# Filler matmuls in TensorE's waits: an attention block and a quantised feed-forward block in one program

## What is computed

```
x = x + attention(layernorm(x), ctx, ctx, Wq, bq, Wk, bk, Wv, bv, Wo, bo)    # 16 heads of 32, RoPE on q and k, causal
x = x + ffn(layernorm(x), w_gate, w_up, w_down)                              # inner size 1536

def act_qdq(x):                                  # one scale for the whole tensor
    scale = jnp.maximum(jnp.max(jnp.abs(x)) / 32767, 1e-12)
    return jnp.clip(jnp.round(x / scale), -32768, 32767) * scale

def ffn(x, w_gate, w_up, w_down):                # lpbq_dequant: 4 bits, one scale for each 32 weights
    x = act_qdq(x)
    up = act_qdq(x @ lpbq_dequant(w_up).T)
    gate = act_qdq(x @ lpbq_dequant(w_gate).T)
    sig = fixed_qdq_u16(jax.nn.sigmoid(gate))
    gate = act_qdq(gate * sig)
    o = act_qdq(gate * up)
    return o @ lpbq_dequant(w_down).T
```

## Time and profile before

| what | us |
|---|---|
| median of three runs | 1491.33 |
| the profiled execution, its own time | 1493.25 |
| its span | 1491.5 |
| TensorE busy with matmuls | 1371.2 (92% of the span) |
| VectorE busy | 1182.0 (79%) |
| ScalarE busy | 968.2 (65%) |
| GpSimd busy | 342.6 (23%) |

### The profile page before, as it was taken

How to read it: one execution, slowest core, us unless ns; L and a number is a source line. 1 busy time by engine, 2 the same in 40 slices (tenths; PEclk the granted TensorE clock), 3 DMA queues, 4 the chain that set the end, 5 groups by cost and what they waited for, 6 DMA issues and landing times.

```text
span 1491.5 us, 24413 instructions
## 1 busy us (share of the span) xinstructions
PE 1371.2 (92%) x9186; PEld 772.7 (52%) x9186; DVE 1182.0 (79%) x1793; ACT 968.2 (65%) x2027; POOL 342.6 (23%) x326
## 2 busy tenths in 40 slices
PE   5899999999999999979999999999999408999999
PEld 4566666667666766643444444444444203444444
DVE  6878888888898888747788987898899899565541
ACT  6988888898888888746422222999889894222210
POOL 0544455444455454430111111000000000000000
PEclk9999999999999999989999999999999758999999
DMA  6111121211121111114533333677689999577632
GB/s 230 48 58 58 65 69 53 72 71 72 72 72 58 58 43 44 37 55 143 190 117 130 134 109 117 234 247 261 240 298 321 388 397 372 201 235 237 236 99 85
DMA packets 101557, 224.75 MB, mean 151 GB/s; under 512 B 8768, under 2 KB 21184, under 8 KB 99776
## 3 DMA queue, kind: packets, MB, share of 16 engines
q1 hardware_dynamic: 100864, 219.00, 41.4%
q10 hardware_dynamic: 576, 4.19, 0.8%
HBM read 140.32 MB, written 82.84 MB: 150 GB/s over the span
## 4 chain that ended last, share of the span: by engine, by line
PE 49%; issue 4%; DVE 1%; ACT 0%; POOLq 0%; POOL 0%
PE ffn_banks L1275 32%; PE ffn_banks L1292 17%; DVE ffn_wide L1484 0%; DVE ffn_peaks L1491 0%; DVE qg L1614 0%; DVE ffn_rises L1489 0%; DVE ffn_wide L1483 0%; ACT qg L1346 0%; ACT ffn_wide L1346 0%; PE ffn_banks L1283 0%; DVE ffn_wide L1645 0%; DVE ffn_wide L1673 0%; ACT ffn_ring L1325 0%; DVE ffn_rest L1612 0%; DVE ffn_peaks L1499 0%
## 5 line engine op out<-in xcount | busy, mean ns | idle before, releaser
L1275 PE MATMUL ffn_banks<-ffn_wide,ffn_rest 128*128 128x512 f16 x2304 | 500.1, 380 | 3.7 <-DVE ffn_wide L1479 2.7
L1275 PEld LDWEIGHTS ffn_banks<-ffn_wide,ffn_rest 128*128 128x128 f16 x2304 | 225.8, 98 | 277.8 <-issue 3.4
L1292 PE MATMUL ffn_banks<-ffn_rest,ffn_wide 128*128 128x512 f16 x1152 | 250.6, 381 | 63.2 <-DVE ffn_wide L1649 63.2
L640 ACT ACTIVATE qg<-score_banks,neg_max 128x128 f32<-128x128 f32 (+1 forms) x512 | 208.2, 450 | 20.8 <-DVE neg_max L512 20.8
L1292 PEld LDWEIGHTS ffn_banks<-ffn_rest,ffn_wide 128*128 128x128 f16 x1152 | 113.0, 98 | 200.8 <-issue 66.1
L1444 ACT ACTIVATE ffn_u_steps<-ffn_ring,ffn_scales 128x1024 int16<-128x1024 f32 x48 | 55.0, 1148 | 153.4 <-DMA ffn_ring<-ups_dram 133.4
L417 POOL TENSOR_TENSOR qg<-qg,per_sum 128x512 f32<-128x512 f32 x64 | 85.9, 1342 | 269.7 <-DVE per_sum L516 269.7
L1346 ACT ACTIVATE ffn_rest<-ffn_banks,ffn_row_back 128x1024 f32<-128x1024 f32 x66 | 73.0, 1105 | 95.2 <-PE ffn_banks L1275 91.5
L419 POOL TENSOR_TENSOR qg<-qg,per_sum 128x1024 f32<-128x1024 f32 x64 | 133.7, 2088 | 0.0
L640 ACT ACTIVATION_READ_ACCUMULATOR qg<-score_banks,neg_max 128x1 f32 x512 | 121.1, 237 | 0.0
L649 ACT ACTIVATE pt<-ring_banks 128x512 f32<-128x512 f32 x128 | 70.4, 610 | 41.9 <-PE ring_banks L776 41.0
(11 more groups left out here) (198 smaller groups left out, 2695.6 us busy)
## 6 DMA issues: line engine op xcount, KB each, us to landing
ffn_ring<-ups_dram SPq DMA_DIRECT2D x44, 512.0 KB, 5.7
ups_dram<-ffn_rest SPq DMA_DIRECT2D x42, 512.0 KB, 3.7
ffn_wide<-ups_dram SPq DMA_DIRECT2D x13, 1024.0 KB, 14.0
gates_dram<-ffn_rest SPq DMA_DIRECT2D x24, 512.0 KB, 2.7
ffn_ring<-gates_dram SPq DMA_DIRECT2D x24, 512.0 KB, 4.6
signs_dram<-qg SPq DMA_DIRECT2D x24, 512.0 KB, 4.2
qg<-signs_dram SPq DMA_DIRECT2D x48, 256.0 KB, 7.2
ffn_rest<-w_parts_dram SPq DMA_DIRECT2D x36, 256.0 KB, 4.4
```

The source lines that it names most:

```text
L640: last = act.activation(prob[:, s % 2, h, lo:hi], score_banks[:, h, lo:hi], ACT.Exp, bias=neg_max[:, s % 2, part, h:h + 1], accum_out=row_ ...
L1275: last = pe.matmul(banks[:, pair_of(s), half, :], w[:, m % 2, wp, c, :], xq[:, xp, n, c, :], start=(k == 0), stop=(k == 3 * DC - 1))
L1292: last = pe.matmul(down_banks[:, g % 2, t, :], oq[:, g % 2, op, m, t * P:(t + 1) * P], w_down[:, wp, wk, c], start=(start and k == 0), sto ...
```

## The change

A function `turn_over(bank, times)` issues so many matmuls one after the other. Each multiplies a 128x128 block of the matrix of ones, read as bfloat16, with 256 columns of the same tile, and writes 256 columns of a PSUM bank that nobody reads before it is written anew. None of them waits for another engine except where written, and none signals one. They stand at six places of TensorE's program, 130 in all: 22 ahead of the first `QK`, 10 ahead of the first `V`, 18 ahead of the last `PT` (after a new wait for the last exponentials), 26 after the last `O`, 18 after the matmul that spreads the input's maximum, and 36 ahead of the down projection (after a new wait for 22 of the 24 product units). In `QK` and `V` the waits are reordered: the wait for a free bank now stands first.

```diff
+        unused = ones[:, :].bitcast(BF16)
...
+            def turn_over(bank, times):
+                for _ in range(times):
+                    pe.matmul(bank, unused[:, 0:P], unused[:, :], start=True, stop=True)
...
                 if name == "QK":
+                    b = open_bank("QK", g, i)
+                    if i == 0 and g == 0:
+                        turn_over(banks[:, b, 0:SEQ], 22)
...
-                    b = open_bank("QK", g, i)
...
                 if name == "V":
+                    b = open_bank("V", g, i)
+                    if i == 0 and g == 1:
+                        turn_over(banks[:, b, 0:SEQ], 10)
...
-                    b = open_bank("V", g, i)
...
                 if name == "PT":
+                    if s == BATCH * GROUPS - 1:
+                        pe.wait_ge(exped, s + 1)
+                        turn_over(score_banks[:, 3, 0:SEQ], 18)
                     pe.wait_ge(normed, s + 1)
...
                     if name == "O":
                         last.then_inc(last_filled, 1)
+                        if g == 1:
+                            turn_over(score_banks[:, 3, 0:SEQ], 26)
...
             pe.matmul(banks[:, 3, 0, 0:P], keep["ones"][:, :], spread, start=True, stop=True).then_inc(top_spread, 1)
+            turn_over(banks[:, 2, 0, 0:2 * P], 18)
...
                 if g < 2:
                     pe.wait_ge(staged, 2 * NP)
+                    if g == 0:
+                        pe.wait_ge(u_peaked, ND - 2)
+                        turn_over(banks[:, 3, 1, 0:2 * P], 36)
```

More of the change, by code:

```diff
@@ L980, in feed_forward @@
         block = ctx.enter_context(nc.Block())
+        unused = keep["ones"][:, :].bitcast(BF16)
         first, second = chain_slots()
```

## The result

| | before | changed |
|---|---|---|
| median of 10 runs | 1491.61 us | 1483.26 us |
| lowest to highest | 1488.55 to 1496.18 | 1482.03 to 1488.15 |
| profiled execution | 1493.25 | 1482.14 |

The ratio is 0.9948, with a 95% interval of 0.9934 to 0.9963: faster by 5 to 10 us. The forecast was 1485.9 with a range of 1482.5 to 1490.3, so the time lies in the range, 2.6 us under the point. The two profiled executions differ by 11.1 us, more than the medians do.

A forecast was written before the change was run, and what follows sets the result against it. TensorE was taken to bound the kernel from 692 us to the end. The terms 1.98 + 1.2 + 1.7 + 0.45 + 0.2 + 1.8 = 7.3 us came off the profiled 1493.25, giving 1485.9, range 1482.5 to 1490.3.

The forecast's parts named there:

- Part 1: 22 fillers ahead of the first QK: QK0 2.2 us shorter, gain capped at 1.98 us by VectorE's wait for ScalarE.
- case of a late rise: Ahead of the first QK: a clock rise 1.2 us later leaves 5 or 6 products cold, gain 1.4 us.
- Part 2: 10 fillers ahead of the first V: V1 at full clock, exponentials sooner, gain 1.2 us, 0 to 1.5.
- Part 3: 18 fillers ahead of the last PT: transposes and Oc at full clock, 1.7 us where the clock fell, otherwise 0.
- Part 4: 26 fillers after the last O: the second four YT transposes at full clock, 0.45 us, or 0.
- The rule of the Trainium skill: At YT's transposes: transpose-mode matmuls don't count as work, so the clock falls after the 26 fillers; sum 6.65, time 1486.6.
- Part 5: Spreading matmul faster if the clock stands, even odds, 0.2 us; the 18 fillers after it worth 0, -0.7 to +0.1.
- Part 6: 36 fillers ahead of the down projection: its first 3.6 us at full clock, gain 1.8 us, up to 2.4.
- The first rival: Attention's rhythm gives back the early gains of 3.2 us: 1489.1 us, chance 0.15.
- The second: Fillers raise the clock but do not hold it; only first QK and down projection gain, 3.8 us: 1489.5, chance 0.1.
- The slow one: At all six places each filler waits for the one before to drain: 10.5 us slower, 1503.7 us, chance 0.05.
- a microsecond that TensorE saves at the head of either stretch is a microsecond of the end: From 692 us: TensorE bounds gate and up products, 477 us, and down projection, 250.6 us, unless another engine sets the head.

The follow-up runs named there:

- e1: The kernel before with only the 22 fillers ahead of the first QK and the 10 ahead of the first V: ratio 0.9977, 3.4 us.
- e3: The kernel before with only the 36 fillers ahead of the down projection: ratio 0.9981, 2.8 us.
- e9: The changed kernel without the 18, 26 and 18 fillers around the border of attention and the feed-forward part: ratio 0.9957.
- e5: The changed kernel with 36 transposes in place of the 36 fillers ahead of the down projection: clock rose 6.0 us after the start; no time given.
- e4: The changed kernel without the 18 fillers after the spreading matmul: ratio 0.9954.
- e8: The changed kernel with 8 more fillers ahead of the last sequence's first PV and 12 ahead of its third S: ratio 0.9941.
- e6: The changed kernel with 72 fillers ahead of the down projection in place of 36: 1486.97 us, one run.
- e7: The changed kernel with 18 fillers ahead of the down projection in place of 36: 1489.41 us, one run.
- e2: The kernel before with only the 18, 26 and 18 fillers around the border of attention and the feed-forward part: ratio 1.0008.
- after_again: The changed kernel measured a second time: ratio 0.9946.
- e10: The changed kernel with 8 and 12 more fillers near the end of attention and 14 ahead of the second sequence's first S: ratio 0.9955.

## Why the prediction was right, and where it was off

1. *Part 1, 1.98 us*: right in size (1.96 at the rotation, 2.1 at 38.6 us) and in mechanism. `QK0` now waits 0.85 us for its operands after the fillers and takes 2.6 us instead of 4.8 (its 24 starts lie between 21.65 and 24.16). The rotation starts with no idle time before it: VectorE's own work ahead of it has become the limit, as the cap of 1.98 us said. The clock rose sooner than the 21.2 us I had put: the fillers' spacing drops from 0.213 to 0.109 us at 19.5, 2.6 us after the first of them (1.5 to 4.3 in the eleven profiles that have the 22). My case of a late rise was added up wrongly: a rise 1.2 us later leaves 3 products cold, not 5 or 6, and a gain of 1.7 us, not 1.4. That the gain is carried to the end is shown by e1.
2. *Part 2, 1.2 us*: mis-sized; the stretch gave 1.7. I let VectorE's wait of 1.23 us for ScalarE cap it. VectorE's reciprocal took all of that (51.01 to 47.59, -3.42), but at 55.00, the next score maximum, the saving was 3.81. That one had waited for TensorE, whose 3.4 us at half clock (43.17 to 46.59) cost it 1.7. I also took the fall at 43 to be one that only some executions have. It came in all three profiles that have no fillers there, at 43.2, 43.5 and 43.6, and in none of the eleven that have them.
3. *Part 3, 1.7 us, where the clock falls*: the size was right to 0.1 us, and so was the condition. Of the three other profiles in which the last `PT` runs without fillers and so could show it (e1, e3, e9), none had a fall there. So a fall came in one of four such profiles, and that the one I added up from had it was luck: for the median, this part was worth less than I put in.
4. *Part 4, 0.45 us*: 0.46, and in every profile: from the last `otlo` to the first instruction of the feed-forward part it is 9.35 or 9.36 us in the four without these fillers, and 8.89 or 8.90 in the ten with them. The clock stood through `YT`'s transposes, and it fell only at 661.3. The rule of the Trainium skill that the prediction weighed ("TensorE: Matmul & The Clock Gate", part 4) had been taken to make this 0; it came out at 0.46. The place itself does not decide on the rule, since the clock fell soon after. e5 does not agree with it: there the clock rose while nothing but float32 transposes ran.
5. *Part 5, 0.2 us and the fillers 0*: 0.31 and 0.1. The 0.31 needs the clock to stand until the spreading matmul has run, and it did so in 3 of the 10 profiles with the 26 fillers (the changed kernel, e4 and e8), in place of the even odds I gave it. e4 shows the cover by VectorE.
6. *Part 6, 1.8 us*: 1.8 (250.6 to 248.8 us busy). e3 shows it alone, e6 the price of a filler beyond the cover, e7 that half the number gave nothing.

The score maximum of point 2, in the kernel before, with its wait for TensorE:

```profile
55.00 0.69 DVE L511 TENSOR_REDUCE neg_max<-score_banks 128x4 f32<-128x512 f32 x1 [1.18 <-PE score_banks L765]
```

The first rival, that attention gives the early gain back, is refuted by e1. The second, that fillers raise the clock but don't hold it, is refuted by the fall at 43, which came without the 10 fillers each time and never with them, and by the 0.46 us of part 4. The slow one, that fillers do not follow each other closely, is refuted by their spacing: the 26 take 3.00 us, 0.109 us from start to start. Its sum held a slip of 0.2 us: 26 x 0.27 is 7.0, 3.3 us late and not 3.1.

One step failed, though the time came out in the range: that from 692 us on "a microsecond that TensorE saves at the head of either stretch is a microsecond of the end". For the first of the two stretches, the pieces, it holds for the profiled execution of before, and for three of the others, not in general. That explains how e2's profile could be 4.3 us ahead after the border and 0.1 at the first product unit, and it puts 1.07 us of loss into the profile of the changed kernel, which the pass over products then happened to give back. Against this went 3.0 us inside attention that I had no term for: 1.7 for a fall at 633.7 which no filler touches and which was absent, and 1.3 gathered in small steps between 55 and 520 us.

The largest of those steps, 0.85 us at 207 us, is one VectorE instruction (L507, L508 in the changed kernel) that took 2.80 us before and 1.96 after, where its median is 0.69. Beside it GpSimd was adding a bias (L405, from 204.66 to 207.02 before; L406, from 199.95 to 202.32 after), and VectorE's instruction ended 0.55 us later than that in both. The 14 profiles hold 162 cases in which this instruction takes over 0.8 us. In each it starts while that addition of GpSimd runs, and ends 0.54 to 0.56 us after it. So VectorE is held until GpSimd is done, and the size of the step is how long GpSimd still had to run (2.26 us before, 1.41 after). The instruction before and after:

```profile
204.76 2.80 DVE L507 SCALAR_TENSOR_TENSOR qg<-turns,sin_turned 128x512 f32<-128x512 f32 x1
200.91 1.96 DVE L508 SCALAR_TENSOR_TENSOR qg<-turns,sin_turned 128x512 f32<-128x512 f32 x1
```

The medians differ by 8.3 us, the ratio gives 7.8 (5.5 to 9.8), and my sum was 7.3, from the profiled execution. What came in every profile that could show it is 1.96 + 1.7 + 0.46 + 1.8 (1.5 to 2.5), or 5.9 us; the 0.4 of part 5 and the 1.7 of part 3 come on top where the clock allows it. That the point lay only 2.6 us from the median is in part luck: it was added up from an execution 1.9 us above the median of before, with a fall that one in four has. And the border's share has not been shown in the times at all: alone it gave -1.2 us (-3.1 to +0.7), in its context 1.6 us with intervals that overlap. The gains measured for the beginning and the down projection alone, 3.4 and 2.8 us, make 6.2; with the border's -1.2 it is 5.0, against 7.8 for all. Each of them is uncertain by 1.6 to 2.2 us, so this gap is not clear of noise.

## What to carry to other kernels

Fill a wait of TensorE only with what ends inside it, and right up to its end: 36 fillers that left 1.5 us saved 1.8 us, 72 cost their excess in full, and 18 that left 3.3 us saved nothing (one execution each of the last two). A saving is local until the next stretch where another chain is close behind: before counting on "TensorE bounds", compare the same stretch over several executions, not one. A fall of the clock in the profile that you add up from may be there in one execution of four: look for it in others too. Where medians can't tell two versions apart, the difference of starts between two traces of the same instruction order gives each step to 0.1 us.

## What was not expected of the hardware

- Float32 transposes alone raised the clock (e5, 1227.9 us, 6.0 us after their start).
- Ahead of the down projection it took 2.6 to 5.1 us from the first filler to the rise, with the same instructions in the same place (3.6 in the changed kernel, 4.9 in after_again, which is the same kernel, and 5.1 in e10).
- VectorE's L507, with a median of 0.69 us, took up to 2.80 when it started beside an addition of GpSimd: it ended 0.55 us after that one, each time.
- Stores of 512 KB seem to set the pass at times: ScalarE waited for stores of signs 5.9 us in all between 900 and 1175 us in the profile of before, 10.5 in that of the changed kernel and 14.6 in e2's, for the same stores.
